# Two adaLN blocks on one core: chunk groups 3, 3, 2, a delta-rule state laid out by key with its sums on TensorE, and late gathers in the second layer's buffers

## The reference

```python
def dpfp(k):                      # 8 values of a head -> 16 features
    x = jax.nn.relu(jnp.concatenate([k, -k], axis=-1))
    phi = x * jnp.roll(x, 1, axis=-1)
    return phi / (jnp.sum(phi, axis=-1, keepdims=True) + EPS)
def step(W, inputs):              # W: [batch, 16 heads, 8 values, 16 features]
    k_i, v_i, q_i, b_i = inputs
    v_bar = jnp.einsum('bhvk,bhk->bhv', W, k_i)
    W = W + jnp.einsum('bhv,bhk->bhvk', b_i * (v_i - v_bar), k_i)
    y = jnp.einsum('bhvk,bhk->bhv', W, q_i)
    return (W, y.reshape(B, H * dk))
```

## Time and profile before

| | |
|---|---|
| median of 3 runs (lowest, highest) | 1880.94 us (1879.56, 1885.45) |
| profiled execution, its span | 1881.02 us, 1878.5 us |
| TensorE busy, weight loads busy | 1385.0 us (74%), 1046.0 us |
| VectorE, ScalarE, GpSimd busy | 1092.9 us (58%), 855.8 us (46%), 840.6 us (45%) |
| mean granted clock of TensorE | 0.851 |
| chain that ended last | PE 39%, DVE 15%, POOL 9%, issue 8%, ACT 7% |

### The profile page before, as it was taken

One profiled execution on the slowest core, in us unless ns is written; L12 is line 12 of the kernel. 1 busy time (PEld: TensorE's weight loads), 2 busy tenths in 40 slices (PEclk: granted clock), 3 DMA queues, 4 the chain that ended last, 5 costly groups with the idle time before them and its releaser, 6 DMA issues.

```text
span 1878.5 us, 29132 instructions
## 1 busy us (share of the span) xinstructions
PE 1385.0 (74%) x8304; PEld 1046.0 (56%) x8304; DVE 1092.9 (58%) x2573; ACT 855.8 (46%) x1811; POOL 840.6 (45%) x826
## 2 busy tenths in 40 slices
PE   2788998846377878777777787785554999945986
PEld 1355555523135666666656667574443777844764
DVE  3677777635626781122766455757688757793144
ACT  1466666634125434464644455643131645312543
POOL 2011111105777761557835743646757451382043
PEclk9999889978679979888887887987786999967998
DMA  7654544349124434343434332423101021111123
GB/s 306 180 146 142 152 137 138 89 156 376 65 69 148 148 119 123 110 120 113 134 93 120 110 89 79 126 73 124 43 20 50 29 68 32 32 43 41 35 78 97
DMA packets 226295, 204.43 MB, mean 109 GB/s; under 512 B 21372, under 2 KB 197269, under 8 KB 223093
## 3 DMA queue, kind: packets, MB, share of 16 engines
q1 hardware_dynamic: 197699, 150.31, 25.8%
q0 software_dynamic: 22528, 42.78, 7.6%
q10 hardware_dynamic: 5938, 9.69, 1.4%
HBM read 95.87 MB, written 106.82 MB: 108 GB/s over the span
## 4 chain that ended last, share of the span: by engine, by line
PE 39%; DVE 15%; POOL 9%; issue 8%; ACT 7%; DMA 1%; SPq 0%; DVEq 0%; POOLq 0%; ACTq 0%
PE psum L1235 6%; PE psum L1305 5%; PE psum L1256 4%; PE psum L1289 4%; PE psum L1379 4%; PE psum L1400 3%; POOL sorted_x L2050 3%; PE psum L1247 3%; POOL w_all L2108 2%; POOL e_gath L2063 2%; ACT e_gath L1523 2%; PE psum L1387 2%; PE psum L1225 2%; PE psum L1156 1%; PE psum L1162 1%
## 5 line engine op out<-in xcount | busy, mean ns | idle before, releaser
L2063 POOL DMA_INDIRECT e_gath<-sorted_y,e_rowsy x256 | 280.7, 1096 | 261.1 <-issue 129.9
L2050 POOL DMA_INDIRECT sorted_x<-h_fm,e_rows x256 | 269.5, 1053 | 121.3 <-issue 77.3
L1770 DVE TENSOR_TENSOR e_a<-psum,e_g 128x176 f32<-128x176 f32 x224 | 75.4, 338 | 312.1 <-ACT e_g L1480 298.8
L1235 PE MATMUL psum<-w_all,e_xd 128*128 x896 | 227.6, 366 | 8.4 <-issue 3.9
L298 DVE TENSOR_REDUCE at_negm<-psum 128x2 f32<-128x512 f32 x256 | 163.2, 684 | 67.6 <-PE psum L174 66.8
L1235 PEld LDWEIGHTS psum<-w_all,e_xd 128*128 128x128 f32 x896 | 160.1, 219 | 43.9 <-issue 37.9
L1305 PE MATMUL psum<-ident,e_prod 128*128 128x128 f32 x640 | 143.2, 388 | 47.1 <-DVE e_prod L1822 47.1
L1305 PEld LDWEIGHTS psum<-ident,e_prod 128*128 128x128 f32 x640 | 141.7, 312 | 48.9 <-DVE e_prod L1822 47.6
L1247 PE MATMUL psum<-ident,e_a 128*88 128x128 f32 x448 | 99.7, 308 | 75.7 <-DVE e_a L1770 37.6
L375 ACT ACTIVATE w_all<-psum 128x512 f32<-128x512 f32 x256 | 141.7, 591 | 26.9 <-PE psum L187 22.3
L1480 ACT ACTIVATE e_g<-psum 128x176 f32<-128x176 f32 x224 | 71.6, 320 | 159.7 <-PE psum L1235 158.4
(11 more groups left out here) (299 smaller groups left out, 2802.9 us busy)
## 6 DMA issues: line engine op xcount, KB each, us to landing
sorted_y<-e_ys SPq DMA_DIRECT2D x134, 256.0 KB, 2.2
e_xt<-sorted_x SPq DMA_DIRECT2D x112, 256.0 KB, 2.7
sorted_x<-zeros SPq DMA_DIRECT2D x10, 2048.0 KB
qk_parts<-at_part SPq DMA_DIRECT2D x96, 192.0 KB, 3.3
at_qs<-qk_parts SPq DMA_DIRECT2D x16, 576.0 KB
at_ks<-qk_parts SPq DMA_DIRECT2D x16, 576.0 KB
sorted_x<-zeros ACTq DMA_DIRECT2D x16, 512.0 KB
w_all<-in_w_all SPq DMA_DIRECT2D x1, 7296.0 KB, 24.2
```

The lines of the kernel that those rows point to most:

```text
L1235: mm = pe.matmul(ps[:, UP[p % 2], i * 256:i * 256 + 2 * HIDDEN], x_d[:, q % 2, t % 4 * P:(t % 4 + 1) * P], w_all[:, ds(offset[t], 2 * HIDD ...
L2050: pool.indirect_dma_start(sorted_x, bass.IndirectOffsetOnAxis(rows0[:, t, k:k + 1], 0), h_tm[:, t * D:(t + 1) * D], None).then_inc(scatter ...
L2063: pool.indirect_dma_start(gath[:, t % GATH, k * D:(k + 1) * D], None, sorted_y[g], bass.IndirectOffsetOnAxis(rows_y[:, t, k:k + 1], 0)).th ...
```

## The change

`GROUP0` becomes chunks 0 to 2, 3 to 5, 6 and 7; the score of group 0 stands after the logits of chunk 2. The scatters of chunks 6 and 7 are due earlier (ticks 24 to 52 instead of 98 to 127). `SORTED` has four groups (0 to 3, 4 and 5, 6, 7), so 96 tiles of the second mixture instead of 88; their results lie one after the other in one table, and GpSimd's second gathers are due in ticks 293, 316 and 333 (`GATHER1`), the last group's after the ticks.

The expert rows of chunks 6 and 7 are gathered into the eight buffers `gathered_rows` of the second mixture, which lie in the space of the first layer's expert weights. Scales have a table of their own (`SCALE`), which for the last two chunks is ahead of `COMBINE`.

`state` and `prod` are laid out by feature, head, value. A product with keys or queries is made in two halves of 8 features; in chunks 0 to 4 and 6 its upper half is then added to its lower half (`fold`, one instruction), in chunks 5 and 7 not (`FOLDS`). What is left, 8 or 16 features, is added up by TensorE: for the keys with the identity as the stationary operand (`key_sum`, tokens stay on partitions), for the queries as before (`query_sum`). `u` is one pair of instructions for both tiles of a step and reads the sum from PSUM. The outer product and the addition take all 2048 elements at once. `y_fm` has the space of the zeros and is copied step by step. All chunks are treated alike; `ticks_of_chunk` gives each piece its tick by its weight, with one tick between a product and what needs its sum.

The two layer norms of the second layer are normalised on ScalarE, from factors that VectorE computes. Seven of eight `turn_back` stand between the last group's tiles, and `result` of a chunk follows the `mix` of the next. All tables of ticks are new; there are 347 ticks.

```diff
+    def dve_factors(self, dve, n):
+
+        v = self.nc.vector
+        dve.wait_ge(self.std, n + 1)
+        v.reciprocal(self.sd[:], self.sd[:]).then_inc(self.norm, 1)
+        dve.wait_ge(self.norm, 3 * n + 1)
+        v.scalar_tensor_tensor(self.sh[:], self.mv[:, :, 0], -1.0, self.sd[:], ALU.mult, ALU.mult).then_inc(self.norm, 1)
+
+    def act_norm(self, act, n):
+        act.wait_ge(self.norm, 3 * n + 2)
+        for t in range(CT):
+            ins = self.nc.scalar.activation(self.nt[:, t, :], self.ps[:, t * P:(t + 1) * P], ACT.Identity,
+                                            bias=self.sh[:, t:t + 1], scale=self.sd[:, t:t + 1])
+        ins.then_inc(self.norm, 1)
+
     def pe_n(self, pe, n):
...
-GROUP0 = ((0, 2), (2, 5), (5, 8))
+GROUP0 = ((0, 3), (3, 6), (6, 8))
...
-SORTED = ((0, 4), (4, 7), (7, 8))
+SORTED = ((0, 4), (4, 6), (6, 7), (7, 8))
...
-BLANK = ROW0[1] // BATCH
-BLANK_LATE = 4096
-BLANKED = (BATCH, BATCH + (ROW0[2] - ROW0[1]) // BLANK_LATE, BATCH + (ROW0[3] - ROW0[1]) // BLANK_LATE)
+BLANK, BLANK_LATE = 1024, 4096
+LATE_ROW = (BATCH * BLANK,) + ROW0[1:]
+BLANKED = tuple(BATCH + (ROW0[g + 1] - LATE_ROW[0]) // BLANK_LATE for g in range(3))
...
+OPENING = (("x", 0), ("x", 1), ("n", 0), ("n", 1), ("l", 0), ("x", 2), ("l", 1), ("n", 2), ("l", 2), ("x", 3), ("score", 0),
+           ("count", 0), ("su", 0), ("rank", 0), ("table", 0), ("n", 3), ("x", 4), ("sd", 0), ("l", 3), ("sx", 0), ("su", 1), ("sd", 1),
...
-Y_ON_PE = 3
-BEGIN = (97, 135, 179, 219, 243, 267, 291, 316)
-STEP = (19, 20, 20, 12, 12, 12, 12, 12)
+BEGIN = (112, 140, 168, 198, 226, 251, 272, 295)
+STEP = (13, 13, 14, 13, 11, 10, 9, 9)
 END = tuple(b + CB * n for b, n in zip(BEGIN, STEP))
...
-GATHER = ((60, 63, 74, 76),
...
-          (245, 247, 255, 262),
-          (268, 271, 280, 284))
...
-X_NEW = (87, 116, 164, 194, 221, 245, 269, 292)
...
-SCATTER1 = (155, 195, 237, 257, 298, 315, 336, 358)
-BEGIN1 = (271, 331)
...
+GATHER = ((93, 100, 102, 106), (107, 110, 115, 118), (131, 134, 139, 142), (164, 167, 173, 175), (191, 192, 198, 202),
+          (208, 217, 222, 225), (227, 230, 233, 236), (242, 245, 249, 251))
+COMBINE = ((90, 93, 98, 101), (112, 115, 119, 125), (137, 144, 145, 148), (169, 172, 176, 179), (198, 198, 205, 210),
+           (221, 224, 230, 231), (254, 255, 256, 256), (273, 274, 274, 275))
+SCALE = ((90, 93, 98, 101), (112, 115, 119, 125), (137, 144, 145, 148), (169, 172, 176, 179), (198, 198, 205, 210),
+         (221, 224, 228, 231), (234, 237, 240, 243), (245, 249, 252, 255))
+X_NEW = (102, 125, 154, 182, 211, 234, 258, 277)
+PROJECT = (108, 131, 160, 188, 217, 240, 264, 283)
+FEATURES = (112, 135, 164, 192, 220, 244, 268, 287)
...
+SCATTER = ((24, 29, 35, 39), (42, 46, 50, 52))
+SCATTER1 = (168, 187, 209, 242, 267, 293, 311, 333)
...
+FOLDS = (1, 1, 1, 1, 1, 0, 1, 0)
...
+SUM_LAG = 1
...
+def pieces_of_chunk(m):
+    def products(op, s, z):
+        return tuple((op, s, z, half) for half in HALVES) + tuple(("fold_" + op, s, z, level) for level in range(FOLDS[m]))
+
+    def update(s):
+        return tuple((op, s, z, 0) for z in range(LT) for op in ("outer", "add"))
+
+    keys = [tuple(x for z in range(LT) for x in products("key", s, z)) for s in range(CB)]
+    return (keys[0] + (("u", 0, 0, 0),) + update(0)
+            + keys[1] + products("query", 0, 0) + (("u", 1, 0, 0),) + products("query", 0, 1) + update(1)
+            + products("query", 1, 0) + products("query", 1, 1))
+
+
+def ticks_of_chunk(m):
+
+    pieces, n = pieces_of_chunk(m), CB * STEP[m]
+    weight = [2 if x[0] in ("outer", "add") else 1 for x in pieces]
+    ticks, last, at = [[] for _ in range(n)], {}, 0
+    for i, (op, s, z, part) in enumerate(pieces):
+        at = max(at, sum(weight[:i]) * n // sum(weight))
+        needs = [("key", s, y) for y in range(LT)] if op == "u" else [("query", 0, z)] if op == "outer" and s > 0 else []
+        at = min(n - 1, max([at] + [last[x] + SUM_LAG for x in needs]))
+        ticks[at].append((op, s, z, part))
+        last[op.replace("fold_", ""), s, z] = at
+    return ticks
...
+def sums_of_chunk(m):
+
+    ticks = ticks_of_chunk(m)
+    last = {}
+    for i, pieces in enumerate(ticks):
+        for op, s, z, _ in pieces:
+            last[op.replace("fold_", ""), s, z] = i
+    last["query", 0, 0] = max(last["query", 0, 0], last["u", 1, 0])
+    sums, tick = [], 0
+    for op, s in (("key", 0), ("key", 1), ("query", 0), ("query", 1)):
+        for z in range(LT):
+            tick = max(tick, last[op, s, z] + SUM_LAG)
+            sums.append((tick, op, s, z))
+    return sums
...
+BEGIN1 = (250, 295, 327)
+GATHER1 = (293, 316, 333)
...
-        state = sb("state", [P, LT, HEADS, DEPTH, KD])
-        prod = sb("prod", [P, LT, HEADS, DEPTH, KD])
+        state = sb("state", [P, LT, KD, HEADS, DEPTH])
+        prod = sb("prod", [P, LT, KD, HEADS, DEPTH])
...
-        y_tm = T["zeros"][:].rearrange("p (t d) -> p t d", d=D)
+        u_of = sb("u", [P, LT, D])
+        y_fm = T["zeros"]
...
+        LATE = CT * GROUP0[2][0]
+        GATH_HOME = [("gath", t % GATH, t - GATH if t >= GATH else None) for t in range(LATE)]
+        GATH_HOME += [("rows", i, None) for i in range(TILES - LATE)]
+        
+        def gath_of(t):
+            kind, i, _ = GATH_HOME[t]
+            return gath[:, i, :] if kind == "gath" else gathered_rows[i]
...
+        BACK_AT = {3 + 2 * m: m for m in range(CHUNKS - 1)}
...
-            def y_sums(m, t):
-                n, z = CB * m + t // LT, t % LT
-                pe.wait_ge(query_prod, 4 * n + 2 * z + 2)
-                if t == 0:
-                    pe.wait_ge(yfm_done, m)
-                for k in range(KD):
-                    mm = pe.matmul(side[:, t * P:(t + 1) * P], prod[:, z, :, :, k].rearrange("p h v -> p (h v)"), ident[:],
-                                   start=(k == 0), stop=(k == KD - 1))
+            def key_sum(m, s, z):
+                n, left = CB * m + s, KD >> FOLDS[m]
+                if FOLDS[m]:
+                    pe.wait_ge(folded, fold_count(m, s, z, "key"))
+                else:
+                    pe.wait_ge(key_prod, 4 * (n - 1) + 2 * z + 2)
+                if s == 0 and z == 0:
+                    pe.wait_ge(yfm_done, CB * m)
+                for k in range(left):
+                    mm = pe.matmul(side[:, (LT + z) * P:(LT + z + 1) * P], ident[:], prod[:, z, k].rearrange("p h v -> p (h v)"),
+                                   start=(k == 0), stop=(k == left - 1))
+                mm.then_inc(vbar_done, 1)
+
+            def query_sum(m, s, z):
+                n, left = CB * m + s, KD >> FOLDS[m]
+                if z == 0:
+                    pe.wait_ge(yfm_done, n)
+                    if s == 0:
+                        pe.wait_ge(u_done, u_count(n + 1) - 1)
+                if FOLDS[m]:
+                    pe.wait_ge(folded, fold_count(m, s, z, "query"))
+                else:
+                    pe.wait_ge(query_prod, 4 * n + 2 * z + 2)
+                for k in range(left):
+                    mm = pe.matmul(side[:, z * P:(z + 1) * P], prod[:, z, k].rearrange("p h v -> p (h v)"), ident[:],
+                                   start=(k == 0), stop=(k == left - 1))
                 mm.then_inc(y_done, 1)
...
+                    for tick, op, i, z in SUMS[m]:
+                        if r == tick and op == "key" and CB * m + i > 0:
+                            key_sum(m, i, z)
+                        if r == tick and op == "query":
+                            query_sum(m, i, z)
...
+            for t in range(FIRST_TILE1[NG1 - 1], FIRST_TILE1[NG1] + 2):
+                stage1(t, FIRST_TILE1[NG1 - 1], TILES1[NG1 - 1])
+                if t - FIRST_TILE1[NG1 - 1] in BACK_AT:
+                    turn_back(BACK_AT[t - FIRST_TILE1[NG1 - 1]])
+            turn_back(CHUNKS - 1)
...
-                        if p == COMBINE[m][i]:
-                            combine(m, i)
+                        if p == SCALE[m][i]:
+                            scale(m, i)
...
+            wide = lambda u: by_head(u).unsqueeze(1).broadcast_to([P, KD, HEADS, DEPTH])
+            tall = lambda key: key.rearrange("p h k -> p k h").unsqueeze(3).broadcast_to([P, key.shape[2], HEADS, DEPTH])
...
+            def piece(m, op, s, z, part):
...
+                    v.tensor_tensor(pr_z[:, ks], st_z[:, ks], tall(keys[:, :, ks]), ALU.mult).then_inc(key_prod, 1)
+                if op == "u":
...
+                        dve.wait_ge(vbar_done, LT * n)
+                        v.tensor_tensor(u, vn, side[:, LT * P:2 * LT * P].rearrange("p (z d) -> p z d", d=D), ALU.subtract).then_inc(u_done, 1)
+                        dve.wait_ge(u_done, u_count(n) - 1)
+                        v.tensor_tensor(by_head_of(u), by_head_of(u), strength, ALU.mult).then_inc(u_done, 1)
...
+                        if s > 0:
+                            dve.wait_ge(y_done, LT * (n - 1) + z + 1)
```

(23 more changed lines are left out.)

233 lines of the change are left out of this document (103 added, 130 removed), and 7 rows, old and new, of the table OPENING.

## The result

The changed kernel takes 1911.8 us (median of 4 runs, 1909.4 to 1912.7), the kernel before in the same series 1880.3: the ratio is 1.0176, with a 95% interval from 1.0145 to 1.0207. The forecast was 1844 with a range of 1770 to 1905. The profiled execution has a span of 1909.9 us.

What follows compares the result with a forecast made beforehand. While expert tiles run, TensorE's stream was taken to set the pace, with stops where it waits for others; afterwards large waits. Terms 23-28+53-104+19 = -37 took 1881 to 1844 us, range 1770 to 1905.

Steps and rivals of the forecast that it cites:

- (a): Start to the first expert tile: groups of 3, 3, 2 chunks make that tile come later, +23 us.
- (b): Ticks 48 to 89: gathers and scales start later, so these ticks hold tiles alone, -28 us.
- (c): Ticks 112 to 223: four recurrences beside expert tiles, TensorE's added work partly filling its idle time, +53 us.
- (d): Last expert tile to last `y_fm`: fewer chunks remain and most waits for gathered rows go, -104 us.
- the load behind the late scatter: Load for tick 295, behind a scatter issued in tick 293: expected as the next late one, some 7 us.
- (e): From the last `y_fm` copy to the end: 96 second-layer tiles instead of 88, +19 us.
- the 34 us stop: TensorE's wait for a second-layer tile's rows, 34.0 us, ascribed to 32 gathers ahead of chunk 6's scatter; would go.
- C: Rival: a chunk costs as much beside the expert tiles as after them, (c) +90, 1881 us; chance 0.10.
- B: Rival: VectorE's 38 waits for TensorE's sums lengthen ticks, 2.6 us each, +100, 1944 us; chance 0.17.
- D: Rival: the layout fails, sums stay at 0.218 us, +60 in (d), +18 in (c), 1922 us; chance 0.06.
- A: Rival: fuller TensorE stays at 2.4 GHz, ticks 112 to 223 take 370 us, not 431; 1783 us; chance 0.20.

Runs made afterwards that it cites:

- the last version: Changed kernel with scales due a tick ahead, and gathers, scatters and three combines moved in ticks 112 to 222: 1842.9 us.
- e4: Changed kernel with one term left in each sum on TensorE in chunks 0 to 3: 1909.6 us.
- e5: Changed kernel with four folds on VectorE instead of one in chunks 0 to 3: 1922.9 us.

## Why the prediction was wrong, step by step

*(a) First tile +23: right in size*, +26 (the first matmul at 586.6 for 583), but in part by luck. The scatters ended about as forecast: the load of the first rows was issued at 579.0 and had landed by 582.0. But TensorE's opening list, for which the prediction had +11, grew by 26 us too: it ran until 582.1 (555.8 before), the same 2.54 us ahead of the first transposes as in the kernel before, whose rows had landed long ahead. So two paths ended together, and only one of them was forecast:
```profile
580.15 1.98 PE L1246 MATMUL psum<-e_ad,e_gath 88*128 88x512 f32 x4 [1.41 <-DVE e_ad L1864]
584.67 1.11 PE L1310 MATMUL psum<-ident,e_xt 128*128 128x128 f32 x4 [2.54 <-issue]
```

*(b) Ticks 48 to 89, -28: right*, -23; these ticks take 97.4/42 = 2.3 us for the 2.2 taken.

*(c) +53: wrong by 40, and this is the step that failed: the overlap.* The prediction summed TensorE's new work (97 to 159 us, middle 128) and let "75 be filled" of its idle time, "since most of it waits on the tile's own steps on other engines". The 128 held 13 us of waits for scales, so the sum stood for 115 us more work and 62 us less idle time. What came is 53 us of work and 40 us of idle time more. Both terms were wrong, and they partly cancel: the work is 62 us less than priced and the idle time 102 more.

The work was overpriced: the sums take 464 instructions at 0.134 us, 62 us, the low end; 5 more combined tiles (17 for 12, not 5.5) take 16, and the tile's own four lines take 249 us where they took 273. The idle time was not filled. Of the 82 us before, 28 were waits at a combine for a scale due in the same tick, and 40 stood before the tile's own transposes, so about half, not most. After, these 40 are 30, so some 10 of the 75 were filled; and the waits for a scale are 69, since each combine brings its stop along. The prediction had priced such a stop at the 2.33 us of the scale and for the added tiles alone, 13 us; the waits grew by 40, because each also got longer, from 28.4/10 = 2.8 to 68.8/16 = 4.3 us.

Three runs carry this. Moving the scales alone takes 24 us off (c), moving gathers, scatters and three combines 35 more, while taking away 401 of TensorE's instructions gives 3. A pair of runs shows the overlap apart from the stops: in the last version against the kernel before with scales ahead (409 and 353 us), TensorE's work is 328 - 275 = 53 us more and its idle time 80 against 78, with 20.5 and 18.9 us of waits for a scale left in each. So here too nothing was filled. That this (c) is +55, like the forecast, is a coincidence of terms; and the kernel before had nothing of its gathers put right. Their totals agree (1843 and 1845) because (b) then brings 11 us and (d) 68. What remains open in (c) is why the ticks that are neither at a combine nor just ahead of one take 0.5 us more than before (3.38 for 2.85); shorter sums on TensorE did not cure it (3.32 in e4), and with more work on VectorE it was worse (3.63 in e5).

*(d) -104: wrong by 30.* Ticks 224 to 249 were priced at 3.7 us "without gather waits"; they took 115/26 = 4.4. The rows of chunks 6 and 7 no longer wait for a combine, but they still pass through GpSimd one at a time, and GpSimd is busy 94 of 115 us there. Curing this order did not shorten (d) as a whole. Shorter sums gave 40 us back for 80, by TensorE's work or by the hand-over. What sets the rest stays open: (d) lay between 409 and 417 us in all other runs of the changed kernel. VectorE's hand-overs, for which some 24 us were taken, are 52.1 + 11.6 + 8.4 = 72 us of waits. Ticks 250 to the last copy took 298 us where 284 were summed; 5 of the 14 are the load behind the late scatter, named as next, which took 12.1 us and not 7:
```profile
PE psum L1466 <- DMA e_xt<-sorted_x: 12.1, 1, 12.1
```
*(e) +19* was +11. The reading that the 34 us stop comes from GpSimd's gathers was right for a third of it.

*The rivals.* C (a chunk costs as much beside the tiles as after them, (c) at +90) had the right size for (c). As a fixed price it doesn't hold, since the order alone took 59 us off; for the 0.5 us in the ticks away from the combines it was not tried. B's waits for sums are 5.8 us in (c); the 52 us of `u` in (d) were not tried apart. The chances had a slip: B and D alone make 0.23, and slower was put at 0.20. D is refuted: the query sums take 34.54/240 = 0.144 us in (c) and 3.57/32 = 0.112 us later, for 0.218 in the old layout. The key operand, which steps 64 bytes from head to head, costs nothing: 1.22 us for 1024 elements against 1.245, and 1.27 for the query product with the same step.

The Trainium skill (Advanced Engine Details and Errata, Memory Cachelines) wants two hits on a line of 16 bytes to hide its latency; both numbers agree with it: 0.218 us for the matmul operand with a step, and 1.22 us for the key that is read eight times over.

*A* asked for a clock that stays high with a fuller TensorE. The clock did follow the work (0.79, 0.84, 0.88 in (c)), and 0.84 for 0.82 was too little to pay for it. The Trainium skill (TensorE: Matmul & The Clock Gate, Part 1: The HAM clock gate) has activity release the slow rate. The three runs agree in direction; the price of a stop shows in the combine behind it, 3.78 for 2.05 us.

## What to carry to other kernels

Where engines run lists in order and a tick is laid out on all of them, price a job by the stop that it puts into the pace-setting engine, not by its instructions: find in the trace what that engine's idle time waits for, and ask whether the new work fills that idle time or brings more of it. Due times that are equal on the producing and the consuming engine are such a stop in every tick; one tick of lead was worth 37 to 39 us in both kernels. It did not end the stop, since much of it moved into the tick that then held the scale; the rows have to be there earlier too. And a queue that carries both transfers and steps of another chain (here GpSimd's gathers and features) must be ordered by when each can start, since whatever waits at its head holds all behind it.

## What the runs showed of the hardware that was not expected

Less work on TensorE bought almost no time in (c): 401 instructions fewer, 54 us at 0.134, took the stretch from 468 to 465 us. TensorE's busy time fell by only 20 us, as the granted clock went from 0.84 to 0.79 and the other instructions took longer, and its idle time rose by 17. 465 instructions more took the clock to 0.88 and the stretch to 483 us. The combine's 16 instructions took 3.78 us behind a stop, at a clock of 0.50, and 2.05 at a clock of 1.00.
